# An audio tower's front convolutions in row tiles of TensorE, and its attention step reordered

## What is computed

```python
y = conv1d(x, w1, b1, stride=1, pad=1)            # 2 -> 16 channels, 3 taps, length 4096
y = maxpool(relu(bn(y)), 8)                       # length 512
y = conv1d(y, w2, b2, stride=1, pad=1)            # 16 -> 64 channels, 3 taps
y = maxpool(relu(bn(y)), 4)                       # length 128
q, k, v = Wq y + bq, Wk y + bk, Wv y + bv         # 8, 8 and 64 channels
y = gamma * (v @ softmax(q^T k)^T) + y            # 128 x 128 attention per row
y = bn(conv1d(y, w3, b3, stride=2, pad=1))        # 64 -> 128 channels, 4 taps, length 64
```

## Time and profile before

| what | value |
|---|---|
| median of three runs | 1342.02 us (1342.01 to 1344.54) |
| profiled execution | 1346.97 us |
| span in its trace | 1345.1 us, 42753 instructions |
| TensorE matmul busy | 1232.2 us, 92% |
| TensorE weight loads | 827.9 us, 62% |
| VectorE, ScalarE, GpSimd busy | 869.1 (65%), 815.5 (61%), 620.6 us (46%) |
| mean granted clock of TensorE | 0.962 of full |
| front (stage 1a), from the timeline | 0 to 111.5 us |
| tower (stage 1b) | 111.5 to 207 us |

### The profile page before, as it was taken

How to read it: one execution, slowest core, us unless ns; L and a number is a source line. 1 busy time by engine, 2 the same in 40 slices (tenths; PEclk the granted TensorE clock), 3 DMA queues, 4 the chain that set the end, 5 groups by cost and what they waited for, 6 DMA issues and landing times.

```text
span 1345.1 us, 42753 instructions
## 1 busy us (share of the span) xinstructions
PE 1232.2 (92%) x15668; PEld 827.9 (62%) x15668; DVE 869.1 (65%) x2952; ACT 815.5 (61%) x2513; POOL 620.6 (46%) x938
## 2 busy tenths in 40 slices
PE   6998997999999997999999998899999999879997
PEld 2445764555555555777777777666666664456665
DVE  3775445777777776787788786555555554746664
ACT  2994545888888884445455455555555556635553
POOL 5001245677676774365556555333333332335555
PEclk9997996999999998999999999899999999969999
DMA  8400000000000000000000000000000000000000
GB/s 229 100 0 1 1 1 1 1 0 0 0 0 0 0 1 1 3 0 0 0 0 0 0 0 2 2 1 0 0 0 0 0 0 1 1 1 19 16 16 17
DMA packets 10318, 14.00 MB, mean 10 GB/s; under 512 B 9232, under 2 KB 9360, under 8 KB 9744
## 3 DMA queue, kind: packets, MB, share of 16 engines
q1 hardware_dynamic: 10256, 13.15, 4.0%
HBM read 11.05 MB, written 2.10 MB: 10 GB/s over the span
## 4 chain that ended last, share of the span: by engine, by line
PE 59%; issue 14%; DVE 10%; POOL 10%; ACT 5%; POOLq 1%; DMA 1%; DVEq 0%; ACTq 0%; SPq 0%
PE bank L1333 7%; POOL big L534 6%; PE bank L1672 5%; PE bank L1690 5%; PE bank L145 5%; PE bank L1328 4%; PE bank L1034 3%; PE bank L1357 3%; PE bank L1061 2%; PE bank L164 2%; PE bank L359 2%; PE bank L1437 2%; PE bank L1102 2%; PE bank L1112 2%; PE bank L1026 2%
## 5 line engine op out<-in xcount | busy, mean ns | idle before, releaser
L534 POOL TENSOR_TENSOR big<-big 128x512 f32<-128x512 f32 x128 | 133.2, 1041 | 59.8 <-DVE big L729 59.8
L698 ACT ACTIVATE big<-big 128x128 f32<-128x128 f32 x384 | 148.9, 394 | 1.3 <-DVE big L741 1.3
L1405 POOL TENSOR_TENSOR big<-g_a,g_b 64x64 f32 x128 | 40.4, 315 | 185.1 <-DVE g_a L1395 185.1
L940 POOL TENSOR_TENSOR big<-big 128x512 f32<-128x512 f32 x64 | 65.7, 1047 | 118.9 <-DVE big L1210 118.9
L641 PEld LDWEIGHTS bank<-cst,big 128*128 128x128 f32 x512 | 57.4, 142 | 73.4 <-issue 61.4
L1726 ACT ACTIVATE big<-bank 128x512 f32<-128x512 f32 x128 | 66.2, 602 | 51.9 <-PE bank L1672 51.9
L741 DVE CUSTOM_DVE_ANT_0 big<-bank,cst 128x128 f32<-128x128 f32 x384 | 88.7, 287 | 13.7 <-issue 13.7
L1593 POOL TENSOR_TENSOR big<-big 128x512 f32<-128x512 f32 x48 | 61.0, 1270 | 76.2 <-DVE big L1796 73.6
L1372 ACT ACTIVATE g_r<-bank,g_bias 128x64 f32<-128x64 f32 x128 | 40.2, 314 | 89.1 <-PE bank L1333 89.0
L595 PE MATMUL bank<-big 32*128 32x512 f32 x256 | 77.9, 660 | 17.8 <-POOL big L528 10.3
L1386 DVE SCALAR_TENSOR_TENSOR g_t<-bank,cst,g_r 128x64 f32<-128x64 f32 x128 | 36.3, 284 | 85.7 <-ACT g_r L1372 85.7
(11 more groups left out here) (269 smaller groups left out, 3356.5 us busy)
## 6 DMA issues: line engine op xcount, KB each, us to landing
big<-x_dram SPq DMA_DIRECT2D x12, 512.0 KB, 8.2
cst<-consts_dram SPq DMA_DIRECT2D x1, 3364.5 KB, 22.4
out_dram<-h SPq DMA_DIRECT2D x8, 256.0 KB, 2.6
cst<-consts_dram SPq DMA_DIRECT2D x3, 256.0 KB
cst<-consts_dram SPq DMA_DIRECT2D x1, 279.5 KB, 2.9
g_ih_exchanged<-consts_dram SPq DMA_DIRECT2D x2, 96.0 KB, 8.1
a_proj_padded<-consts_dram SPq DMA_DIRECT2D x8, 2.0 KB
cst<-consts_dram SPq DMA_DIRECT2D x8, 2.0 KB
```

Of the source, the lines that this page charges most:

```text
L534: nc.gpsimd.tensor_tensor(P, P, a_rs[t % 4].unsqueeze(2).to_broadcast([128, 4, 128]), ALU.mult).then_inc(a_n_r, 1)
L698: m = nc.scalar.activation(P, raw, ACT.Exp, bias=a_mx[tb % 4][:, k:k + 1], scale=-1.0, accum_out=a_sm[tb % 4][:, k:k + 1])
```

## The change

- **Image layout.** `xin` has 128 partitions: rows g = 0 in partitions 0 to 47, g = 1 in 64 to 111, loaded by six loads per image instead of three; the first image comes in two halves.
- **Convolution 1** (`conv1`) issues two matmuls of 48 partitions, one in each 64-row tile of the array, for the same 512 columns, into two banks. The unit of work is now half an image (h from 0 to 7), four such pairs each. ScalarE copies the first pair's sums to SBUF (`copy1`), from where VectorE takes their maximum; the other three are read from PSUM as before.
- **Convolution 2** (`conv2`) reads the relu's output directly (`h1`, 128 partitions, padded), at three shifts: 3 taps x 4 row tiles of 32 partitions, accumulated in four banks. The three shifted copies by ScalarE are gone; the weights `w2q` lie four times in SBUF, by 12 small loads. VectorE takes its maximum in two instructions of 1024 columns instead of four of 512.
- **Order in the front**: the loops are written out; TensorE does pairs 0 to 2 of half h, then convolution 2 of job h - 2, then pair 3; VectorE the maxima 2 of job h - 3, then the four maxima 1 of half h. Some setup of stage 3 moves: the rows behind the maxima of half 7, two copies to ScalarE, two multiplications to GpSimd as one.
- **Convolution 3** is done for every step, with two row tiles of 64 partitions and 128 columns, 4 taps, in the banks that also hold the values; h is written per step.
- **Order in the tower**: slot s has energies and values of s, transposes of s - 2, convolution 3 of s - 5, attended of s - 3, queries/keys of s + 2. VectorE's reciprocal moves to the end of its slot; weights and sums have three buffers instead of two. The maximum is one instruction instead of two. The product for the projection's bias, its addition and the mixing of stage 3's weights stand in slots -2 and -1.

The diff, cut to its core:

```diff
-    xin = [big1[0:96, 0:LEN], big1[0:96, LEN:2 * LEN]]
+    xin = [big1[:, 0:LEN], big1[:, LEN:2 * LEN]]
...
-    taps = big2[0:96, 2048:2048 + 8 * 512].rearrange("p (k n) -> p k n", k=8)
+    h1 = big2[:, 3072:3072 + 4 * 514].rearrange("p (k n) -> p k n", k=4)
+    c1_copy = big2[:, 5128:5128 + 1024]
+    w2q = cst[:, ON["w1"][0]:ON["w1"][0] + 384]
...
+        def conv1(h, k):
+            i, q = h // 2, 4 * (h % 2) + k
+            if q == 0:
+                pe.wait_ge(x_loaded[i % 2], 96 * (i // 2 + 1))
+            elif i == 0 and q == 4:
+                pe.wait_ge(x_half, 18 * 16)
+            if k == 2:
+                pe.wait_ge(c1_copied, h + 1)
+            elif k == 3:
+                pe.wait_ge(c1_max, 4 * h + 2)
...
+            for g in range(2):
+                r = slice(64 * g, 64 * g + 48)
+                m = nc.tensor.matmul(conv1_banks(k)[:, 512 * g:512 * (g + 1)], w1s[r, :], xin[i % 2][r, 512 * q:512 * (q + 1)],
+                                     start=True, stop=True)
+            m.then_inc(c1_sum, 1)
+        def conv2(j):
+            pe.wait_ge(h1_ready, j + 1)
+            if j:
+                pe.wait_ge(c2_max, 2 * j)
+            for t in range(3):
+                for p in range(4):
+                    r = slice(32 * p, 32 * p + 32)
+                    m = nc.tensor.matmul(T(1, p), w2q[r, 128 * t:128 * (t + 1)], h1[r, j % 4, t:t + 512], start=(t == 0), stop=(t == 2))
+            m.then_inc(c2_sum, 1)
+        pe.wait_ge(w_scaled, 2)
+        for h in range(HALVES):
+            if h < JA:
+                for k in range(3):
+                    conv1(h, k)
+            if h == 2:
+                pe.wait_ge(w_scaled, 3)
+            if h >= 2:
+                conv2(h - 2)
+            if h < JA:
+                conv1(h, 3)
+            elif h == JA:
+                pe.wait_ge(c1_max, 4 * JA)
                 pe.wait_ge(loaded, 16)
                 setup3_first_pe(pe)
...
+        def max1(h, k):
+            i, q = h // 2, 4 * (h % 2) + k
+            if k:
+                v.wait_ge(c1_sum, 4 * h + k + 1)
             else:
+                v.wait_ge(c1_copied, h + 1)
+            sums = conv1_banks(k) if k else c1_copy
+            nc.vector.tensor_reduce(h1raw[i % 2][:, :, 64 * q:64 * (q + 1)], sums.rearrange("p (g n k) -> p g n k", g=2, k=8),
+                                    X, ALU.max).then_inc(c1_max, 1)
+        def max2(j):
+            v.wait_ge(c2_sum, j + 1)
+            for k in range(2):
+                nc.vector.tensor_reduce(h2raw[j % 2][:, 256 * k:256 * (k + 1)], T(1, 2 * k, 2).rearrange("p (n k) -> p n k", k=4),
+                                        X, ALU.max).then_inc(c2_max, 1)
...
+        for h in range(HALVES + 1):
+            if h >= 3:
+                max2(h - 3)
+            if h < JA:
+                for k in range(4):
+                    max1(h, k)
+            if h == 1:
+                scale2()
+            elif h == 4:
+                v.wait_ge(loaded, 16)
+                v.wait_ge(b_w, 1)
...
+            elif h == JA - 1:
+                setup3_rows_dve(v)
+            elif h == JA:
                 setup3_middle_dve(v)
...
+        def copy1(h):
+            act.wait_ge(c1_sum, 4 * h + 1)
+            if h:
+                act.wait_ge(c1_max, 4 * h - 3)
+            nc.scalar.copy(c1_copy, conv1_banks(0)).then_inc(c1_copied, 1)
+        def relu1(j):
+            act.wait_ge(c1_max, 8 * (j // 2) + 8)
+            if j >= 4:
+                act.wait_ge(c2_sum, j - 3)
+            nc.scalar.activation(h1[:, j % 4, 1:513], h1raw[j // 2 % 2][:, j % 2, :], ACT.Relu, bias=bn_t[:, 0:1]).then_inc(h1_ready, 1)
...
+        for h in range(HALVES + 1):
+            if h < JA:
+                copy1(h)
+            if h >= 2 and h % 2 == 0 and h <= JA:
+                relu1(h - 2)
+                relu1(h - 1)
+            if h == JA + 1:
+                setup3_copies_act(act)
+            if h >= 3:
+                relu2(h - 3)
...
+        def values(d):
...
+            for p in range(2):
+                m = nc.tensor.matmul(bank(2 + p)[:, 256:384], h2all[:, 2 * d + p, :], c("wv"), start=True, stop=True)
+            m.then_inc(b_vp, 1)
...
-        def conv3(g, half):
-            if not half:
-                pe.wait_ge(b_h3, 2 * g + 2)
-                pe.wait_ge(b_h, g + 1)
-            for k in range(4 * half, 4 * half + 4):
-                m = nc.tensor.matmul(bank(5)[:, 256 * (k // 4):256 * (k // 4 + 1)], c("w3", 128 * k, 128 * (k + 1)),
-                                     h3g[g % 2][:, :, k % 4:k % 4 + 127:2], start=(k % 4 == 0), stop=(k % 4 == 3))
-            if half:
-                m.then_inc(b_c3, 1)
+        def conv3(d):
+            pe.wait_ge(b_h3, d + 1)
+            pe.wait_ge(b_v, min(d + 6, ND))
+            if d:
+                pe.wait_ge(b_h, d)
+            for tap in range(4):
+                for k in range(2):
+                    r = slice(64 * k, 64 * k + 64)
+                    m = nc.tensor.matmul(bank(2 + k)[:, 0:128], c("w3", 128 * (4 * k + tap), 128 * (4 * k + tap + 1))[r],
+                                         h3p[d % 4][r, :, tap:tap + 127:2], start=(tap == 0), stop=(tap == 3))
+            m.then_inc(b_c3, 1)
         pe.wait_ge(b_w, 5)
+        pe.wait_ge(f_dve, 11)
         for s in SLOTS:
-            here, ahead = 0 <= s < ND, s + 1 < ND
-            if here:
-                pe.wait_ge(b_qk, s + 1)
-                if s:
-                    pe.wait_ge(b_exp, s)
+            if 0 <= s < ND:
                 energies(s)
-            if ahead:
-                if here:
-                    pe.wait_ge(b_v, s + 1)
-                for p in range(2):
-                    m = values(s + 1, p)
-                m.then_inc(b_vp, 1)
-                if s >= 3:
-                    pe.wait_ge(b_h3, s - 2)
-                qk(s + 1)
-            if 1 <= s <= ND:
-                transposes(s - 1)
-            for half in range(2):
-                g = group(s, 4 + half)
-                if g is not None:
-                    conv3(g, half)
+                values(s)
             if 0 <= s - 2 < ND:
-                attended(s - 2)
+                transposes(s - 2)
+            if 0 <= s - 5 < ND:
+                conv3(s - 5)
+            if 0 <= s - 3 < ND:
+                attended(s - 3)
+            if s + 2 < ND:
+                qk(s + 2)
+            if s == -2:
+                setup3_middle_pe(pe)
+                nc.tensor.matmul(bank(2)[:, 0:128], c("a_bv"), c("a_p"), start=True, stop=True).then_inc(a_pb_ps, 1)
+            elif s == -1:
+                pe.wait_ge(c2_max, 2 * JA)
+                pe.wait_ge(a_pb_r, 1)
+                pe.wait_ge(f_dve, 13)
...
...
+            if s == -1:
+                for t in h3p:
+                    nc.vector.memset(t[:, :, 0:130:129], 0.0).then_inc(pads_zero, 1)
+                v.wait_ge(a_pb_ps, 1)
+                nc.vector.tensor_tensor(a_pb[:, :], bank(2)[:, 0:128], c("a_bp"), ALU.add).then_inc(a_pb_r, 1)
+                setup3_mixed_dve(v)
...
...
+            if 0 <= s < ND:
+                v.wait_ge(b_exp, s + 1)
+                nc.vector.reciprocal(brs[s % 3], bsum[s % 3]).then_inc(b_rs, 1)
...
...
+            sp.dma_start(cst[:, 0:front], consts[:, 0:front]).then_inc(conv_loaded, 16)
...
+            def x_load(i, a, b, to):
+                for g in range(2):
+                    for t in range(3):
+                        sp.dma_start(xin[i % 2][64 * g + 16 * t:64 * g + 16 * t + 16, a:b],
+                                     xp[i, :, a + t:b + t].rearrange("(c s) n -> c s n", c=2)[:, 8 * g:8 * g + 8, :]).then_inc(to, 16)
+            x_load(0, 0, LEN // 2, x_loaded[0])
+            x_load(0, LEN // 2, LEN, x_half)
+            o = AT["w2"][0]
+            for p in range(4):
+                for t in range(3):
+                    sp.dma_start(w2q[32 * p:32 * p + 32, 128 * t:128 * t + 128], consts[32 * t:32 * t + 32, o:o + 128]).then_inc(x_half, 16)
             for i in range(JA // 2):
                 if i >= 2:
-                    sp.wait_ge(c1_max, 8 * (i - 1) + 2)
-                for t in range(3):
-                    sp.dma_start(xin[i % 2][32 * t:32 * (t + 1), :], xp[i, :, t:t + LEN]).then_inc(x_loaded[i % 2], 16)
+                    sp.wait_ge(c1_sum, 8 * (i - 1))
+                if i:
+                    x_load(i, 0, LEN, x_loaded[i % 2])
                 if i == 1:
                     same = AT["m_w1"][0]
                     sp.dma_start(cst[:, front:same], consts[:, front:same]).then_inc(loaded, 16)
                     experts7_load(sp)
```

More of the change, by code:

```diff
@@ L122, in build @@
+    h3p = [t.rearrange("p (r n) -> p r n", r=2) for t in big2_bufs(4132, 2 * 130, 4)]
     wqk, qkb = sb("wqk", [128, 128]), sb("qkb", [128, 3])
     JA = 8
-    def turns(engine, per, turn):
-        with engine.Fori(0, JA // per - 1) as i:
-            for g in range(per):
-                turn(i, g)
-        for g in range(per):
```

(36 more changed lines are left out.)

292 lines of the change are left out of this document (123 added, 169 removed).

## The result

The changed kernel takes **1408.67 us** (1407.2 to 1410.47), the kernel before beside it 1342.29: a ratio of 1.0491, 95% interval 1.0473 to 1.0509. The change makes the kernel 4.9% slower, and the forecast of 1318 us missed it by 91 us and in its sign.

What follows compares the result with a forecast made beforehand. TensorE was taken to bound front and tower. Gains of 15.1 us up to the first energies, 5.2 in tower steps, 3.4 in the drain and 0.3 in the last copy sum to 24.0: 1342.02 becomes 1318, range 1304 to 1336.

Steps and rivals of the forecast that it cites:

- the start: Front: the image's half lands by about 8 us, so TensorE starts at 8.9 instead of 11.43.
- about 1 for the third image: Front, halves 3 to 7: about 1 us lost as the third image queues behind the large constants on SyncE.
- the late-image rival: Front: third image's loads stuck behind the large constants, some 10 us more, total 1328 us; chance 0.05.
- ring: Front: cycle of convolution 2, VectorE's maxima and convolution 1's fourth pair waiting on each other, 7.65 us a half.
- The slower one: Front: convolution 2's tiles do not run together, 10.2 us each, total 1370 us at least; chance 0.07.
- those of part overlap: Front: convolution 2's four tiles overlap partly, 3.3 us, total 1325, chance 0.08; or only pairs, 5.1 us, 1341, chance 0.05.
- The first rival: Front: the whole TensorE saving of 34 us arrives, total 1295 us; chance 0.05.
- The low clock: Front: TensorE, busy only 6.0 of 7.65, runs at low clock, 10.9 us a half, total 1334 us; chance 0.12.
- second convolution, full clock: Front: 24 records in four row tiles running together take 2.56 us plus 0.2, so 2.76.
- the tail: End of the front: VectorE's setup and maxima in series with two low-clock second convolutions of 5.3 us, 27.6 us in all.
- beat of a half: Front: each half image takes 7.65 us, hand-overs included, five of them 38.3 us.
- last maximum of the first convolution ends: Front: halves 3 to 7, with small operations and the third image's delay, end at 71.4 us.

Runs made afterwards that it cites:

- 128-row loads: The kernel with both load fixes, its taps laid out beforehand as 128 rows (32 of them zeros), one load writing 128 partitions: 1313.98 us, ratio 0.9804.
- both load fixes: The changed kernel with whole rows outermost, 48 partitions in one load, and small loads issued behind the third image: 1322.61 us, ratio 0.9860.

## Why the prediction was wrong

**The step that failed** is in the start: "The image's half is six loads, there by about 8." I counted the loads' issue time and took their transfer for that of before, whose three loads came from the same DRAM rows. The diff showed another view of them, two channels outermost, and I didn't price it. TensorE started at 21.11 instead of 8.9. The same view made the others late too: "about 1 for the third image" was 25.2 (the wait at 114.22), and to the late-image rival I gave 0.05 and 10 us. For the second half image (8.82), the second image (26.98) and the fourth (10.85) the sum had no term at all. The rival was sized with before's rate. At the measured 54 to 56 GB/s an image's 1.57 MB take 28 to 29 us, against a ring that wants one every 15.2; the front is then bound by loads, whatever TensorE does. The first energies came at 187.89 against 101.6 forecast, 86.3 us later; the later start and the excess of the four waits add up to 83.1 of them. Of the rest the tower gained 3.3 more than forecast and what stands behind it lost 4.5. That is 87.5, as the profiled execution's 1410.5 is over its forecast of 1323; the 91 of the medians has 3 more because before's profiled execution lay further above its median than the changed kernel's did.

**The rivals.** The slower one fell, and with it those of part overlap: four row tiles do run together. The forecast's sign was lost to a mechanism that none of them named: the late-image rival had the right engine waiting, but not the view. The first rival's 1295 doesn't come out of its own terms: 34 us of the front and 8.9 of the tower give 1299. The low clock did not hold for the whole ring, but for parts of it. With 128-row loads the granted clock is 0.73 and 0.59 from 20 to 30 us, and 1.00 from 30 to 60, with TensorE busy 8.0 of the last 10. The forecast had taken from the earlier trace rows that a gap of 1.5 us lost the clock; the row itself still has 1.00, and in the trace it falls to 0.50 by 101 us. What such a gap does is not fixed: in every changed kernel whose second convolutions alternate TensorE waits 1.53 us once in the ring, and the product behind it took 2.86 us in four of the traces (with 128-row loads, for one) and 4.55 in five others (with both load fixes, for one). One of the five is the kernel with its third convolution in one tile, which up to there is the same program as the one with 128-row loads, so it is not the program that decides. What does is not shown.

**The terms of the sum**, where their work was fed, from the changed kernel and the one with 128-row loads:

| term | forecast | measured |
|---|---|---|
| second convolution, full clock | 2.76 | 2.79 to the next instruction |
| the same, cold in the tail | 5.3 | 5.10 and 4.55; 4.85 and 4.49 with 128-row loads |
| beat of a half | 7.65 | 7.60 |
| start, with 128-row loads (and the weights' loads of neighbouring rows) | 8.9 | 7.96 |
| last maximum of the first convolution ends, 128-row loads | 71.4 | 73.5 |
| from there to the first energies | 30.2 | 26.2; 25.9 with 128-row loads |
| steady step of the tower | 4.15 | 3.90 |
| third convolution | 1.2 | 1.12 to the next |
| idle ahead of the third convolution, forecast as the wait for the values' copy | 0.2 | 0.17, put down to issue |

The tail in its parts, on VectorE and TensorE of the changed kernel:

```profile
160.53 1.23 DVE L193 TENSOR_REDUCE big<-bank 128x128 f32<-128x1024 f32 x1 [0.72 <-PE bank L153]
...
165.34 2.35 DVE L201 TENSOR_REDUCE big<-bank 128x256 f32<-128x1024 f32 x2
...
167.84 5.10 PE L164 MATMUL bank<-big,cst 32*128 32x512 f32 x24 [7.36 <-DVE big L201]
...
175.12 1.40 DVE L882 SCALAR_TENSOR_TENSOR fX<-cst,bank 64x512 f32<-64x512 f32 x2 [7.42 <-PE bank L917]
176.55 2.36 DVE L201 TENSOR_REDUCE big<-bank 128x256 f32<-128x1024 f32 x2
...
179.05 4.55 PE L164 MATMUL bank<-big,cst 32*128 32x512 f32 x24 [4.06 <-DVE big L201]
...
187.89 0.50 PE L375 MATMUL bank<-big 32*128 32x128 f32 x8 [0.61 <-DVE f_bout_diagonal L898]
```

Preparations 3.7, maxima 2.4, the cold convolution 5.1, middle 1.4, maxima 2.4: as forecast. The setup's products took 2.2 (172.88 to 175.1) where I had 3.6. That is the clock and not the two column tiles in turn: it was granted at 0.79 from 172 to 173 and at 1.00 from 173 to 175, and in the kernel with its second convolution tile by tile the same products, at a granted clock of 0.50, took 3.9 (124.03 to 127.9). The second cold convolution got part of a higher clock; and the last leg (maxima's end at 186.0 to 187.89) was 1.9, not 2.6.

**The tower**: 12.3 us in the kernel with 128-row loads against 8.9 forecast (10.9 against the other trace of the old tower, that with 96-row loads, which took 89.6 us). The energies' way from first to last is 9.4 shorter (56.4 for 65.9), where I had 5.2: the step is 0.25 shorter than forecast, since the other products take 2.61 instead of 2.74, and the first five intervals take 17.8 instead of 19.1, which I had left as they were. The rest, drain and last copy, gains 2.8 for 3.7.

**Behind the tower** I had forecast nothing, and nothing is what these runs can show: the same instructions take 1131.1 us in the kernel before with 96-row loads, 1134.9 with 128-row loads, 1137.4 in before and 1141.9 in the changed kernel, with TensorE's busy time between 1043.1 and 1054.1. So single profiles scatter by as much as the 4.5 us of the ledger.

With loads that keep up the change gives about what was forecast: by medians 1339.38 - 1313.98 = 25.4 us against 24.0. That the two are so close is in part luck. The front gained 17.3 in the profiles (15.1 forecast, and 1 of it is the weights' loads) and the tower 10.9 to 12.3 (8.9 forecast), which is more than the medians show.

## What to carry to other kernels

A load's price is read from both of its views before anything else is costed: how many rows its outermost dimension has (two here, and two engines worked) and how many partitions it writes. Where a change makes an engine faster, work out how often it will want its next input, and set that against the measured rate of loads of exactly that shape. And what a load is queued behind counts as much as its own length: here eight small loads, stuck behind a large one, held an image for 13 us.

## What the runs showed of the hardware

The rate of the image loads by the shape of one load, in windows where images are all or nearly all that moves:

| outermost rows, partitions written | busy share of 16 engines | GB/s |
|---|---|---|
| 2 channels, 16 partitions (changed) | 0.13 to 0.16 | 48 to 57 |
| 2 channels, 32 partitions | 0.13 | 54 to 55 |
| 8, 8 | 0.50 to 0.54 | 79 to 92 |
| 16, 16 | 0.87 to 1.26 | 105 to 151 |
| 16, 48 | 1.03 to 1.16 | 157 to 197 |
| 32, 32 (before) | 0.97 to 1.05 | 210 to 225 |
| 96, 96 | 0.93 to 0.99 | 213 to 223 |
| 128, 128 | 0.96 to 0.97 | 355 to 415 |

A full busy share is not a full rate: the engines were as busy at 131 GB/s as at 370. The Trainium skill (SBUF — State Buffer, "Door 1: The DMA port swizzle") says that a transfer's rate is limited by how many of the memory's 16 inlets its partitions reach, 4 for partitions 0 to 15, 8 for 0 to 31, 16 for 0 to 127, at some 27 GB/s each. The rows for 32 and 128 partitions agree. Most windows of the loads of 16 are above its 109 GB/s, perhaps because loads of neighbouring partitions follow each other, which is not shown. The row for 96, no better than 32, isn't explained by the count, nor is it known why 48 moved less than 32.

Four row tiles of 512 columns, alternating, take 2.79 us for 24 records, against 10.3 in turn (24 records of 0.43): 3.7 times. That is more than the 3.07 times which the forecast quoted from the Trainium skill (TensorE: Matmul & The Clock Gate, part 3), and the measurement decides. Two row tiles of 64 rows and 128 columns take 1.19 us for 16 records, and 2.07 with the tiles removed: 1.7 times.
